# Attention stages with two buffers by tile parity, one exponential per half, its copy on GpSimd and rows normalised by ScalarE

## The reference

```
x = x + tanh(g_xattn[0]) * L0_xattn(layernorm(x), ctx)    # 16 heads of 16, biases, then relu MLP 256-512-256
x = x + tanh(g_ffn[0])   * L0_ffn(layernorm(x))           # gated FFN, 704 wide, operands rounded to FP4 in blocks of 16
x = x + tanh(g_xattn[1]) * L1_xattn(layernorm(x), ctx)    # 16 heads of 16, mask, then projection Wo
x = x + tanh(g_ffn[1])   * L1_ffn(layernorm(x))           # 8 experts, two for each token

# in both attentions
q = layernorm(x) @ Wq;  k = ctx @ Wk;  v = ctx @ Wv       # split into heads
attn = softmax(q k^T / 4)                                 # over the 77 context rows
out  = attn @ v
```

## Time and profile before

| | |
|---|---|
| median of 3 runs | 812.79 us (811.97 to 815.10) |
| the profiled execution | 812.68 us, its span 810.9 us |
| busy in the span | PE 605.9 us (75%), DVE 577.4 (71%), ACT 360.8 (44%), POOL 226.8 (28%) |
| mean granted clock of TensorE | 0.891 |

### The profile page before, as it was taken

The page is one execution under the profiler, slowest core; times in us unless marked ns, Lnnn a source line. Parts: engine busy times, 40 slices in busy tenths (PEclk is TensorE's granted clock), DMA queues, the critical chain, the costliest instruction groups (busy, mean ns, idle before and its releaser), DMA issues.

```text
span 810.9 us, 16662 instructions
## 1 busy us (share of the span) xinstructions
PE 605.9 (75%) x5545; PEld 534.7 (66%) x5545; DVE 577.4 (71%) x1215; ACT 360.8 (44%) x892; POOL 226.8 (28%) x191
## 2 busy tenths in 40 slices
PE   5538778779921269988886679999865399999970
PEld 3237777769921168877775568888765288999960
DVE  5966667647879879999997267787746694555547
ACT  2335665653200244544442245655625355555530
POOL 3343333440028100000001024334320355555530
PEclk9999999989975579999999689999965599999995
DMA  7020000000030000000000000000039312222219
GB/s 215 1 59 2 1 2 2 2 2 1 1 107 0 0 1 0 0 0 0 0 1 1 0 1 2 1 2 2 2 121 377 114 40 80 80 78 74 79 46 311
DMA packets 27626, 36.62 MB, mean 45 GB/s; under 512 B 4024, under 2 KB 22265, under 8 KB 27438
## 3 DMA queue, kind: packets, MB, share of 16 engines
q1 hardware_dynamic: 23822, 25.56, 9.8%
q0 software_dynamic: 3744, 10.23, 4.1%
HBM read 26.47 MB, written 9.31 MB: 44 GB/s over the span
## 4 chain that ended last, share of the span: by engine, by line
PE 32%; DVE 21%; issue 6%; ACT 2%; DMA 2%; DVEq 1%; POOL 0%; SPq 0%; ACTq 0%; POOLq 0%
PE ps L1351 8%; PE ps L1352 7%; PE ps L1353 7%; PE ps L1452 3%; PE ps L1725 2%; DVE fhs L737 2%; DVE fh L767 2%; DVE x_sb L953 2%; DVE fha L746 1%; DVE fha L745 1%; PE ps L1667 1%; PE ps L1421 1%; DVE el_w L830 1%; PE ps L1661 1%; PE ps L1702 1%
## 5 line engine op out<-in xcount | busy, mean ns | idle before, releaser
L1002 POOL TENSOR_TENSOR p_lo<-prob,p_hi 128x616 f16<-128x616 f32 x64 | 87.3, 1364 | 166.0 <-ACT prob L1117 162.5
L1125 ACT ACTIVATE pT<-ps 128x512 f32<-128x512 f32 (+1 forms) x96 | 50.8, 533 | 43.2 <-PE ps L1437 43.1
L581 DVE TENSOR_REDUCE smax<-ps 128x8 f32<-128x616 f32 x64 | 50.8, 794 | 19.4 <-PE ps L1353 13.0
L586 DVE TENSOR_TENSOR prob<-ps,smax 128x308 f32<-128x308 f32 x128 | 55.3, 474 | 7.3 <-POOL p_lo L1002 3.0
L983 POOL TENSOR_TENSOR rstd<-mv,eps_col 128x16 f32<-128x16 f32 (+2 forms) x6 | 1.3, 210 | 207.0 <-DVE mv L475 207.0
L1049 POOL DMA_INDIRECT y_rows<-rn,dst_row x39 | 43.1, 1106 | 56.1 <-DVE rn L932 54.9
L1351 PE MATMUL ps<-kbd_hi,q_hi 128*128 128x308 f32 x128 | 50.3, 393 | 10.7 <-DVE q_lo L570 9.3
L464 DVE CAST ehT_hi<-ehid 128x512 fp32r<-128x512 f32 x39 | 16.7, 428 | 53.1 <-ACT ehid L1328 53.1
L1045 POOL DMA_INDIRECT xin<-x_rows,src_row x39 | 38.1, 978 | 52.6 <-DVE dst_row L899 41.1
L1452 PE MATMUL ps<-vbd_flat,pT 128*128 128x34 bf16 (+1 forms) x1600 | 48.1, 184 | 5.9 <-ACT pT L1125 4.5
L1452 PEld LDWEIGHTS ps<-vbd_flat,pT 128*128 128x128 f16 x1600 | 46.1, 98 | 8.9 <-ACT pT L1125 6.4
(11 more groups left out here) (281 smaller groups left out, 2054.6 us busy)
## 6 DMA issues: line engine op xcount, KB each, us to landing
el_w<-in_L_ffn_W_dram SPq DMA_DIRECT2D x16, 512.0 KB, 9.8
eh_w<-y_rows SPq DMA_DIRECT2D x16, 256.0 KB, 5.5
x_sb<-in_x_dram SPq DMA_DIRECT2D x4, 512.0 KB, 8.5
x_rows<-rn SPq DMA_DIRECT2D x4, 512.0 KB, 9.5
out_dram<-x_sb SPq DMA_DIRECT2D x16, 128.0 KB, 4.0
stage<-in_L_xattn_W_dram SPq DMA_DIRECT2D x2, 512.0 KB, 4.0
eb<-in_L_ffn_b_dram SPq DMA_DIRECT2D x1, 1024.0 KB, 9.8
w<-in_L_ffn_w_down_dram SPq DMA_DIRECT2D x1, 704.0 KB, 7.2
```

Source lines behind the costliest of these rows:

```text
L581: ch.link(dve.tensor_reduce(top.rearrange("p (b h) -> p b h", h=HPB), sc, AX.X, ALU.max))
L586: ins = dve.tensor_tensor(dst[:, one].rearrange("p (h m) -> p h m", m=M), sc[:, k], bcast(top[:, k * HPB:(k + 1) * HPB], 2, M), ALU.subtract)
L1002: pool.tensor_tensor(p_lo[:, c], prob[:, c], p_hi[:, c], ALU.subtract).then_inc(s["lo"], 1)
L1125: act.activation(dst, ps[:, 4 + g % 2, 0:(c[g + 1] - c[g]) * P // 2], ACT.Copy).then_inc(s["pev"], 1)
```

## The change

- `prob`, `p_hi`, `p_lo` and the query parts get a second buffer, chosen by the parity of the tile or of the pair. The waits that guarded the single buffers look back one tile or pair further.
- ACT computes one exponential for each half, in place in `prob`. POOL copies it to the 16-bit `p_hi` and then subtracts as before (`two_halves`).
- The normalisation of x goes from DVE to ACT: scale by the inverse deviation and add a shift, which POOL computes for all tiles in two small instructions (`shift_rows`) ahead of the barrier before each attention. It runs at the end of ACT's even step, a pair ahead.
- The steps of PE, ACT and DVE are in another order. DVE does both halves of the shift first. ACT does both exponentials first, then the evictions, with `x_high` between them. PE takes `x_transpose` and the first half of the scores ahead of the second group of transposes, `query` ahead of the projection, and the values last.
- Query parts are split in the same even step as they are made; before, `q_low` stood in the odd step.

```diff
-        prob = sb("prob", [P, HM], F32, work)
-        p_hi = sb("p_hi", [P, HMP], F16, work)
-        p_lo = sb("p_lo", [P, HMP], F16, work)
+        prob = sb("prob", [P, 2, HM], F32, work)
+        p_hi = sb("p_hi", [P, 2, HMP], F16, work)
+        p_lo = sb("p_lo", [P, 2, HMP], F16, work)
...
-                def normalise(p):
-                    att_wait(dve, n, "xt", p)
-                    for k in range(2):
-                        t = 2 * p + k
-                        ins = dve.tensor_scalar(xn[:, k], x_sb[:, t], mv[:, 2 * n, t, 0:1], rstd[:, 2 * n, bass.ds(t, 1)],
-                                                ALU.subtract, ALU.mult)
-                    ins.then_inc(s["xn"], 1)
...
-                def softmax_shift(t, h):
+                def softmax_shift(t, par, h):
...
-                    att_wait(dve, n, "lo", 2 * (t - 1) + h + 1)
-                    dst = prob[:, h * HM // 2:(h + 1) * HM // 2]
+                    att_wait(dve, n, "lo", 2 * (t - 2) + h + 1)
+                    dst = prob[:, par, h * HM // 2:(h + 1) * HM // 2]
...
-                def step(t, pair=None, query=None, back=True, front=True):
+                def step(t, par, pair=None, pair_par=0, back=True, front=True):
                     if front:
-                        softmax_shift(t, 0)
+                        softmax_shift(t, par, 0)
+                        softmax_shift(t, par, 1)
                     if back:
                         norm(t - 2)
-                    if front:
-                        softmax_shift(t, 1)
+                    if pair is not None:
+                        x_low(pair)
                     if back:
                         o_low(t - 2)
-                    if query is not None:
-                        q_low(query)
                     if pair is not None:
-                        normalise(pair)
+                        q_low(pair, pair_par)
                     if back and n:
                         residual(t - 2)
-                    if pair is not None:
-                        x_low(pair)
-                    if back and n:
                         att_wait(dve, n, "res", t - 1)
                         moments(t - 2)
 
-                ch.done(dve.memset(p_hi[:, HM:], 0.0))
-                ch.link(dve.memset(p_lo[:, HM:], 0.0))
-                dve.wait_ge(rs[2 * n], 1 + n)
-                normalise(0)
+                ch.done(dve.memset(p_hi[:, :, HM:], 0.0))
+                ch.link(dve.memset(p_lo[:, :, HM:], 0.0))
                 x_low(0)
-                q_low(0)
-                step(0, pair=1, back=False)
-                step(1, query=1, back=False)
-                per = 6 + 2 * n
-                with dve.Fori(0, 6) as i:
+                q_low(0, 0)
+                step(0, 0, pair=1, pair_par=1, back=False)
+                step(1, 1, back=False)
+                per = 2 * (6 + 2 * n)
+                with dve.Fori(0, 3) as i:
                     ch.loop(i, per)
-                    step(2 * i + 2, pair=i + 2)
-                    step(2 * i + 3, query=i + 2)
-                ch.end(6, per)
-                step(14)
-                step(15)
+                    for k in range(2):
+                        step(4 * i + 2 * k + 2, 0, pair=2 * i + k + 2, pair_par=k)
+                        step(4 * i + 2 * k + 3, 1)
+                ch.end(3, per)
+                step(14, 0)
+                step(15, 1)
                 if n:
                     aggregate(3, last=EARLY)
-                step(16, front=False)
-                step(17, front=False)
+                step(16, 0, front=False)
+                step(17, 1, front=False)
...
+            def shift_rows(k, n, part):
+                pool.wait_ge(rs[n], part)
+                ch.link(pool.tensor_tensor(shift_a[:, k], mv[:, n, :, 0], rstd[:, n], ALU.mult))
+                pool.tensor_scalar(shift_a[:, k], shift_a[:, k], -1.0, None, ALU.mult).then_inc(rs[n], 1)
...
-            def low_parts(n, t):
+            def two_halves(n, t):
 
                 s = att_s
                 for h in range(2):
                     att_wait(pool, n, "exp", 2 * t + h + 1)
+                    if h == 0:
+                        att_wait(pool, n, "pt", 3 * (t - 1))
+                    c = slice(h * HM // 2, (h + 1) * HM // 2)
+                    pool.tensor_copy(p_hi[:, t % 2, c], prob[:, t % 2, c]).then_inc(s["hi"], 1)
                     att_wait(pool, n, "hi", 2 * t + h + 1)
-                    c = slice(h * HM // 2, (h + 1) * HM // 2)
-                    pool.tensor_tensor(p_lo[:, c], prob[:, c], p_hi[:, c], ALU.subtract).then_inc(s["lo"], 1)
+                    pool.tensor_tensor(p_lo[:, t % 2, c], prob[:, t % 2, c], p_hi[:, t % 2, c], ALU.subtract).then_inc(s["lo"], 1)
...
+                def normalise(p):
+                    att_wait(act, n, "xt", p)
+                    for k in range(2):
+                        t = 2 * p + k
+                        ins = act.activation(xn[:, k], x_sb[:, t], ACT.Identity, bias=shift_a[:, n, bass.ds(t, 1)],
+                                             scale=rstd[:, 2 * n, bass.ds(t, 1)])
+                    ins.then_inc(s["xn"], 1)
...
-                    att_wait(act, n, "scores", 4 * p)
+                    att_wait(act, n, "scores", 4 * (p - 1))
...
-                def exp(t, h):
-
-                    if h == 0:
-                        att_wait(act, n, "lo", 2 * t)
-                        att_wait(act, n, "pt", 3 * t)
+                def exp(t, par, h):
+
                     att_wait(act, n, "shifted", 2 * t + h + 1)
                     c = slice(h * HM // 2, (h + 1) * HM // 2)
-                    act.activation(p_hi[:, c], prob[:, c], ACT.Exp).then_inc(s["hi"], 1)
-                    act.activation(prob[:, c], prob[:, c], ACT.Exp).then_inc(s["exp"], 1)
+                    act.activation(prob[:, par, c], prob[:, par, c], ACT.Exp).then_inc(s["exp"], 1)
...
-                def step(t, pair=None, front=True, mid=True, back=True):
+                def step(t, par, pair=None, pair_par=0, ahead=None, front=True, mid=True, back=True):
+                    if front:
+                        exp(t, par, 0)
+                        exp(t, par, 1)
                     if mid:
                         p_out(t - 1, 0)
+                    if pair is not None:
+                        x_high(pair)
+                    if mid:
+                        p_out(t - 1, 1)
+                        p_out(t - 1, 2)
                     if back:
                         o_high(t - 2)
-                    if mid:
-                        p_out(t - 1, 1)
-                    if front:
-                        exp(t, 0)
-                    if mid:
-                        p_out(t - 1, 2)
-                    if front:
-                        exp(t, 1)
                     if pair is not None:
-                        x_high(pair)
-                        q_high(pair)
-
+                        q_high(pair, pair_par)
+                    if ahead is not None:
+                        normalise(ahead)
+
+                act.wait_ge(rs[2 * n], 2 + n)
+                normalise(0)
                 x_high(0)
-                q_high(0)
-                step(0, pair=1, mid=False, back=False)
-                step(1, back=False)
-                with act.Fori(0, 6) as i:
-                    step(2 * i + 2, pair=i + 2)
-                    step(2 * i + 3)
-                step(14)
-                step(15)
-                step(16, front=False)
-                step(17, front=False, mid=False)
+                normalise(1)
+                q_high(0, 0)
+                step(0, 0, pair=1, pair_par=1, ahead=2, mid=False, back=False)
+                step(1, 1, back=False)
+                with act.Fori(0, 2) as i:
+                    for k in range(2):
+                        step(4 * i + 2 * k + 2, 0, pair=2 * i + k + 2, pair_par=k, ahead=2 * i + k + 3)
+                        step(4 * i + 2 * k + 3, 1)
+                step(10, 0, pair=6, pair_par=0, ahead=7)
+                step(11, 1)
+                step(12, 0, pair=7, pair_par=1)
+                step(13, 1)
+                step(14, 0)
+                step(15, 1)
+                step(16, 0, front=False)
+                step(17, 1, front=False, mid=False)
...
                 def step(t, col, pair=None, back=True, mid=True, more=True):
                     if mid:
                         p_transpose(t - 1, 0)
-                    if back:
-                        o_transpose(t - 2)
-                    if mid:
-                        p_transpose(t - 1, 1)
-                        p_transpose(t - 1, 2)
-                    if back and n:
-                        project(t - 2)
                     if pair is not None:
                         x_transpose(pair)
                     if more:
                         scores(t + 1, 1 - col, 0)
                     if mid:
-                        values(t - 1)
```

(12 more changed lines are left out.)

39 lines of the change are left out of this document (21 added, 18 removed).

## The result

The changed kernel takes **846.74 us** (median; 842.49 to 847.61) against 812.38 for the kernel before on the same chips: ratio 1.0406, 95% interval 1.0364 to 1.0449. The profiled execution took 847.02 us, its span 845.3. The forecast of 845 holds.

The account below looks back on a forecast made before the run. Hand-overs between engines in fixed orders were taken to bound the first attention, PE nearly alone the second. 812.7 + 2.9 + 20.2 + 4.4 + 1 + 4 = 845 us, range 835 to 856.

Parts of the forecast that it names:

- First stage: Tiles 2 to 13 of the first attention: 15.63 us a pair against 15.14, +2.9 us over six pairs.
- The walk: One pair of tiles followed through the new engine orders, each term once: 15.63 us in attention 0, 18.76 in attention 1.
- Second stage: Tiles 2 to 13 of the second attention: 18.76 us a pair against 15.40, +20.2 us over six pairs.
- The projection's wait: Second attention, odd step: DVE's residual waits for the projection, which starts only after the late low part, 1.17 us more.
- Ends: Steps without a pair and last tiles of each attention: 0 in the first, +4.4 us in the second.
- Copy on GpSimd: The 16-bit copy in both attentions, taken as 0.7 us each; up to 1.9 us nothing moves, so 0.
- Normalisation: Moved from DVE to the end of ACT's even step, where ACT waits anyway; about 0.7 us, cost 0.
- Entries: Start of each attention: two small GpSimd instructions ahead of the barrier, x's rows ready earlier; +1 us for both.
- clock: PE's waits in both attentions bring stretches at the low clock level: +4 us, bounds 0 and 13.8.
- hand-overs: Gaps between engines within a pair, read to 0.03 us each: 0.3 us a pair in the forecast's range.
- Rival 2: Second attention: DVE's residual finds its projection done, 2.31 us of a pair go, 18 less, 827 us; 12 in 100.
- Rival 1: Both attentions: DVE's second shift precedes the previous tile's transposes, ACT's order costs nothing; 789 us, or 804; 8 in 100.

Follow-up runs that it names:

- the mended order: The changed kernel with only ACT's step reordered: first eviction, x_high, exponential 0, second eviction, exponential 1, third eviction, output's high part; 819.14 us, ratio 1.0070.
- the mixed run: The changed kernel with the mended order in the first attention and the second attention as in the kernel before; 803.15 us, ratio 0.9898.

## Why the prediction was right

**The mechanism** is the one given: ACT's order merges two loops into one. Taken away it gives back 27.6 us, put alone into the old orders it costs 89 us against the same kernel without it (905.36 against 816.29).

**First stage.** The walk, the prediction's sum along the loop, gave 15.63 us a pair; the one pair at full clock took 15.69. Its parts were off by more, in both directions: the double shift took 3.29 us (128.81 to 132.10) and not 3.42, the query until ACT's copy 1.82 and not 1.70, and at the turn of DVE's loop the next reduction came 0.53 after the low part (134.69 to 135.22) and not 0.33. Tiles 2 to 13 took 97.23 us in place of 6 x 15.69 = 94.1. Of these 3.1 us some 0.9 belong to the first pair whatever the clock (14.91 against 13.97 in the mended order, at 1.00); the rest goes with the clock, most of it in one pair of 17.08 us at 0.90.

```profile
102.45:119.53 17.08, 13.09 (x184) 11.84 (x184) 9.88 (x21) 8.37 (x17) 7.94 (x9) 0.90 0.01 2
119.53:135.22 15.69, 11.57 (x184) 10.36 (x184) 9.96 (x22) 8.37 (x17) 8.21 (x9) 1.00 0.00 1
```

**Second stage.** 18.76 us predicted; 18.54 for the pair at 527.45, (600.88 - 508.73) / 5 = 18.43 for the last five. Mis-sized by 0.2 to 0.3: residual and moments take 0.96 us on DVE behind q_low (536.53 to 537.49), not the 1.14 read from the earlier trace rows, where 0.17 more stood ahead of the next reduction, at the turn of DVE's loop. The projection's wait was 1.18 for the 1.17 worked out. The stage came to +19.6 for the +20.2 of the sum, but with a first pair of 19.80 us, 1.4 above the others, that was in no term.

**Ends.** Attention 0: 20.16 for 20.7. Attention 1: 29.30 for 27.7, at a granted clock of 0.84 for which the term had nothing.

**Copy on GpSimd, 0.** Right, and doubled still right; 0.70 us was the value taken. **Normalisation, 0.** ACT does wait behind it in the changed kernel (1.57 us after the row at 127.88), and in the mended order the time is the same with either engine (ratios 1.0070 and 1.0058). But the reason given, that ACT waits there anyway, holds only where the loop leaves it that wait: in the order of before the same 1.08 us cost 5.7 us. The price taken from DVE, about 0.7, was too low by 0.35.

**Entries and clock, 1 + 4.** Entries came to about 0: +0.9 for attention 0, and for attention 1 +0.8 up to its first reduction and -1.8 from there. The clock's 4 lie for some 2 us in attention 0 and for a part in the last end. Between the attentions 2.8 of the +3.6 us fell in code that did not change, which was in no term. This code took 272.2 to 276.4 us in the profiles of all fourteen kernels, and 276.4 is the changed kernel's, so these 2.8 us look like scatter from one execution to the next, though no run settles it. The total was met with errors of both signs: that it came within 2 us is luck, that it came within the range is not.

**What was off on paper.** The range does not follow from its two parts: 4 less and 9.8 more for the clock and 3.6 either way for hand-overs make 837 to 859 and not 835 to 856. Rival 2 counts 2.31 us a pair, the wait of 1.17 and the 1.14 of residual and moments, which DVE must do in any case; with the wait alone it would have been about 836 and not 827. Neither changes the forecast.

**What the prediction did not see:** that PE's and DVE's new orders, the double shift and the one exponential have a gain in them, 1.1 us a pair in attention 0, as soon as ACT's order lets it out. Rival 1 named a related condition (a second shift that is done before the evictions are due) and priced it at 789 to 804; the mended kernel, whose first two evictions do not stand behind that shift, came to 819, since attention 1 is slower than before in it.

The Trainium skill (Perfetto Trace Analysis, Optimizing Scalar/DVE Operations) says that moving some work from DVE to Scalar may make sense if DVE is saturated. Here DVE was not (10.43 of 14.63 us), and the move alone cost 0.66% (0.44 to 0.88). That is in keeping with the condition; no run here has a saturated DVE.

## What to carry to other kernels

Where engines run hand-written orders, what an instruction waits for matters less than what is queued behind it: ACT's evictions needed nothing of the second exponential and were late by it all the same, through three engines. Before an engine is relieved, find the loop that sets the pace; the exponential taken off ACT was worth nothing in one order and 8 us in another. And an order that is good for one stage need not be for the next, even where both are one function: choosing it for each gave the only two versions that were faster than the kernel before (803.15 and 804.83 us).

## What the runs showed of the hardware

- On GpSimd the cast of 616 columns from f32 to f16 takes 0.70 us (64 of them, mean 696 ns), half of the two-input subtraction of the same columns (1,357 ns).
- Two activations of 128 x 256 with scale and bias columns take 1.08 us on ACT; DVE's two-operation form of the same work took 0.73 with GpSimd idle, and 1.60 to 1.71 in five of six places in attention 0 of the mixed run with the rows on DVE, where GpSimd was casting and subtracting beside it; the cause is not tested.
- TensorE's granted clock was lower where PE waited longer, though a wait's length alone does not tell where: it was 1.00 over twelve tiles of the mended order (waits of up to 1.15 us in the pairs read), 0.81 over those with ACT's late evictions (1.5 to 2.6 us), and in the kernel before, like pairs stood at 1.00 and at 0.89. At 0.81 PE was busy for 82.3 us, against 72.4 at 0.96 with the same matmuls.
